# Reordering the first phase of a two-phase Mamba and attention kernel, with the moments of one norm moved from VectorE to ScalarE

## Chip, cores and metric

One NeuronCore of one Trainium2 chip. The metric is the device time of one execution in microseconds (us), lower is better. TensorE (PE), VectorE (DVE), ScalarE (ACT), GpSimd (POOL) and the DMA queue of SyncE (SP) run their own instruction streams and meet only at semaphores.

## The reference

Eight sequences of 512 tokens with 256 channels, all float32. Cut to what matters:

```
h  = layernorm(x, ln1_g, ln1_b)                        # "front" and x + h
xz = rmsnorm(h, rms_w) @ in_proj_w;  xi, z = split(xz) # "mid"
xc = silu(conv4(xi) + conv_b)
delta = softplus((xc @ x_proj_w)[:64] @ dt_proj_w + dt_proj_b)
scan over t: s = exp(delta*A) * s + delta*xc*B ;  y = sum(s*C) + D*xc
x  = x + h + (y * silu(z)) @ out_proj_w                # "back"
x  = x + relu(layernorm(x) @ w1 + b1) @ w2 + b2
g  = layernorm(x)                                      # "gate": an LSTM-like cell,
c  = sig(f)*c + sig(i)*tanh(..)                        # its state c runs from batch to batch
out term tanh(g @ wo + c @ uo + bo)
```

The second phase does attention (two units of eight heads for each batch) and a second pass of the same gate; at the end every batch's output is `x + tanh(xwo + c @ uo + bo)`.

## The kernel before

Everything is ordered by hand. The first phase (`sp_first`, `dve_first`, `act_first`, `pool_first`, `pe_first`) is a software pipeline: iteration `i` (0 to 9) runs the scan of batch `i` in 16 units `u`, and puts the other stages of its neighbours beside them at fixed `u`: `mid` of batch `i+1`, `front` (first norm) of `i+2`, `back` (output projection, FFN) of `i-1` and `gate` of `i-2`. Front exists for `i` = 0 to 5, gate from `i` = 2.

A scan unit is: POOL multiplies `ddb` by `bcb` into `hb` (`bx`, L1078, run three units ahead), ACT writes the exponentials to PSUM (`decay`, L872, one unit ahead), DVE scans (L615) and multiplies by C (L618; in units 4 and 12 POOL does it), and after four units PE sums over states (`sums`, L1199). `decay` of a unit waits until DVE has finished the unit two before it.

PE's matmuls of the other stages write to a ring of three PSUM banks (`first_uses`): the n-th use waits until the use n-3 has been read by its reader. In order: xi 2, out 2, gturn 2, xwo 2, gi 2, z 2, bturn 2, xp 1, FFN ... So `z`'s second half waits for ACT's reading of `gi`'s first (`gate_i`), the transposes `bturn` wait for the second `gi` and the first `z`, `xp` for the second `z`.

The moments of the first norm (`front_moments`) are on DVE at `u` = 6: four `bn_stats` (L501) and four `bn_aggr` (L505). POOL then makes the powers (`front_power`, L1027 to L1033), ACT applies them (`front_apply`, L783). The back norm has the same shape: DVE moments at `u` = 2, POOL `norm_power` (L1043 to L1048) at `u` = 2, ACT `back_apply` (L876) at `u` = 3, PE `bturn`, ACT `back_turned` (L888) at `u` = 6, then the FFN matmuls. POOL holds its large operations back during some of DVE's (the waits on `conv_ok`, `xc_ok`, `sz_ok`); `front_scale` (L1052, L1054) and DVE's `mid_soft` (L600, L602) had no such wait.

At the end DVE adds the final state term to `out_xwo` of each batch (`out_sum`, L1757, L1763), ACT takes the tanh, DVE adds it to `x` (`out_add`, L1769), SP stores.

## Time and profile before

| | us |
|---|---|
| median of 3 runs | 1586.55 (1586.42 to 1591.01) |
| the profiled execution, its time | 1584.47 |
| its span, first to last instruction | 1582.7 |
| PE busy | 1365.7 (86%) |
| DVE busy | 1195.4 (76%) |
| ACT busy | 880.1 (56%) |
| POOL busy | 674.7 (43%) |
| granted TensorE clock, mean | 0.939 |

The profile is of one execution; its own time is 2.1 us under the median and its span 1.8 us under its time. The first phase takes about the first 805 us. A busy share is an average over phases with different limits, so the table says little on what a change in one iteration is worth. Granted clock 1.00 is TensorE at 2.4 GHz, 0.50 at 1.2 GHz.

### The profile page before, as it was taken

To read this page: it belongs to the slowest core of one execution; us is meant where nothing else is said; L and a number is where in the kernel's file an instruction comes from. 1 tells how busy PE (TensorE), PEld (TensorE's weight loads), DVE (VectorE), ACT (ScalarE), POOL (GpSimd) and SP (SyncE) were. 2 spreads that over 40 slices of the span, in tenths; PEclk is the share of its full clock that TensorE was granted. 3 is DMA by queue.
4 is the path that set the end of the run, shared out by engine and by line. 5 is a ranking of instruction groups with operands and counts; after the bars stand their busy time and mean duration, and the time that the engine had idled before them with its cause. 6 is when DMAs were issued, how large, how long until landed. Compare 5 with 4: busy or idle time off the path is not lost.

```text
span 1582.7 us, 17383 instructions
## 1 busy us (share of the span) xinstructions
PE 1365.7 (86%) x5554; PEld 667.0 (42%) x5554; DVE 1195.4 (76%) x1861; ACT 880.1 (56%) x1514; POOL 674.7 (43%) x394
## 2 busy tenths in 40 slices
PE   7434889999999989799976989999999999999994
PEld 2102444545354545455541234454545444444442
DVE  5898999999999999880157878686877777776226
ACT  6465768585767665533112565656565655555633
POOL 2486979697978976731405131213022112100000
PEclk9666989999999999899986899999999999999997
DMA  6524161606161524300225352424343432330144
GB/s 209 188 72 169 60 206 42 215 29 212 55 213 55 186 69 140 100 14 27 66 79 128 79 122 52 99 49 106 71 95 71 95 78 62 75 69 2 42 157 136
DMA packets 93803, 158.05 MB, mean 100 GB/s; under 512 B 8608, under 2 KB 74720, under 8 KB 90592
## 3 DMA queue, kind: packets, MB, share of 16 engines
q1 hardware_dynamic: 93712, 156.94, 34.5%
q8 instruction: 45, 0.74, 0.2%
q14 instruction: 46, 0.38, 0.1%
HBM read 110.91 MB, written 46.01 MB: 99 GB/s over the span
## 4 chain that ended last, share of the span: by engine, by line
PE 59%; DVE 22%; issue 10%; ACT 4%; DMA 2%; POOL 2%; SPq 0%; DVEq 0%; POOLq 0%; ACTq 0%
PE psum L1149 24%; PE psum L2131 8%; PE psum L2065 7%; PE psum L2039 6%; PE psum L2054 5%; DVE psum L615 5%; DVE mx L1526 4%; PE psum L2009 4%; PE psum L1199 2%; DVE middle L579 1%; DVE hb L615 1%; POOL hb L1078 1%; DVE hb L618 1%; DVE bg_stats L501 1%; PE psum L1182 1%
## 5 line engine op out<-in xcount | busy, mean ns | idle before, releaser
L1526 DVE TENSOR_REDUCE mx<-psum 128x1 f32<-128x512 f32 x512 | 343.7, 685 | 151.6 <-PE psum L2039 150.4
L1785 ACT ACTIVATE pw<-psum 128x512 f32<-128x512 f32 x512 | 302.1, 598 | 274.2 <-PE psum L2054 270.8
L1078 POOL TENSOR_TENSOR hb<-ddb,bcb 128x1024 f32<-128x1024 f32 x127 | 309.4, 2458 | 79.8 <-DVE middle L579 55.4
L615 DVE TENSOR_TENSOR_SCAN psum<-psum,hb 128x512 f32<-128x512 f32 x224 | 261.6, 1213 | 26.6 <-ACT psum L872 15.8
L2039 PE MATMUL psum<-kp,qp 96*128 96x512 bf16 x512 | 203.7, 403 | 31.2 <-DVE mx L1526 21.4
L872 ACT ACTIVATE psum<-ddb,A_neg 128x512 f32<-128x512 f32 x256 | 165.3, 680 | 77.9 <-DVE hb L618 55.8
L2054 PE MATMUL psum<-qp,kp 99*128 99x512 bf16 x512 | 197.6, 387 | 5.0 <-ACT pw L1785 4.3
L1947 POOL TENSOR_TENSOR rstd<-rstd,neg_half 128x4 f32<-128x4 f32 x16 | 16.3, 1017 | 414.9 <-DVE rstd L1511 414.9
L618 DVE TENSOR_TENSOR hb<-psum,bcb 128x1024 f32<-128x1024 f32 x112 | 137.1, 1224 | 3.9
L2065 PE MATMUL psum<-pw,v_sb 128*32 128x512 f32 x1024 | 124.2, 602 | 0.5 <-ACT pw L1785 0.5
L1149 PE MATMUL psum<-back,w 128*128 128x512 f32 x256 | 115.3, 605 | 8.3 <-ACT back L888 8.3
L2039 PEld LDWEIGHTS psum<-kp,qp 96*128 96x128 bf16 x512 | 50.4, 99 | 143.1 <-DVE mx L1526 65.3
L2054 PEld LDWEIGHTS psum<-qp,kp 99*128 99x128 bf16 x512 | 49.5, 97 | 123.9 <-issue 91.2
L1199 PE MATMUL psum<-hb,sel 128*32 128x512 f32 x512 | 70.2, 672 | 32.4 <-DVE xc L627 22.3
L1149 PE MATMUL psum<-w,gate 128*128 128x256 f32 x384 | 88.1, 379 | 0.0
L1149 PE MATMUL psum<-late,wx 128*128 128x512 f32 x184 | 87.1, 596 | 0.0
L1149 PE MATMUL psum<-c_state,uh 128*128 128x512 f32 x184 | 86.5, 592 | 0.0
L2131 PE MATMUL psum<-second,wx 128*128 128x512 f32 x168 | 86.0, 592 | 0.0
L2131 PE MATMUL psum<-c_state,uh 128*128 128x512 f32 x168 | 85.8, 591 | 0.0
L1149 PEld LDWEIGHTS psum<-back,w 128*128 128x128 f32 x256 | 48.1, 192 | 75.0 <-issue 58.9
L1149 PEld LDWEIGHTS psum<-w,gate 128*128 128x128 f32 x384 | 73.0, 190 | 9.9
L1149 PE MATMUL psum<-front,w_in 128*128 128x512 f32 x128 | 62.6, 628 | 12.4 <-ACT late L915 8.8
(226 smaller groups left out, 2161.9 us busy)
## 6 DMA issues: line engine op xcount, KB each, us to landing
ddb<-dd SPq DMA_DIRECT2D x64, 512.0 KB, 6.7
bcb<-bc SPq DMA_DIRECT2D x32, 512.0 KB, 7.0
parts<-parts_sb SPq DMA_DIRECT2D x96, 128.0 KB
qp<-parts SPq DMA_DIRECT2D x32, 256.0 KB, 7.8
dd<-dd_out SPq DMA_DIRECT2D x7, 1024.0 KB, 4.8
kp<-parts SPq DMA_DIRECT2D x16, 384.0 KB, 4.6
x_back<-x_dram SPq DMA_DIRECT2D x9, 512.0 KB, 5.1
xh_back<-xh SPq DMA_DIRECT2D x8, 512.0 KB, 3.8
```

The source lines that it names most:

```text
L615: e.tensor_tensor_scan(to[:, g, :], a[:, g, :], h[:, g, :], 0.0, ALU.mult, ALU.add).then_inc(scan_ok, 1)
L618: e.tensor_tensor(h, a, bcb[q][:, 1, :, :], ALU.mult).then_inc(hc_dve, 1)
L872: e.activation(dA[n % 2][:, g, :], ddb[k % NSLOT][:, 0, :], ACT.Exp, scale=A_neg[:, a:a + 1]).then_inc(dA_ok, 1)
L1078: e.tensor_tensor(hb[n % NHB], ddb[k % NSLOT][:, 1:2, :].to_broadcast([P, 2, L]), bcb[q][:, 0, :, :], ALU.mult).then_inc(bx_ok, 2 if n == ...
L1149: ins = e.matmul(to, l, r, start=k == 0, stop=k == len(terms) - 1)
L1199: ins = e.matmul(bank(4)[jj * EB:(jj + 1) * EB, :], sel, h[:, g, :], start=(q == 0 and g == 0), stop=(q == 1 and g == 1))
L1526: used.up(e.tensor_reduce(mx[u % 2][:, n:n + 1], score_bank(used.n), AXIS.X, ALU.max))
L1785: e.activation(pw[n % NPW], bank(5 + n % 2), ACT.Exp, scale=HD ** -0.5).then_inc(exp_ok, 1)
L2039: used.up(e.matmul(score_bank(used.n), qp[u % 3][0:NROW, h, t * P:(t + 1) * P], kp[u % 3][0:NROW, h, :], start=True, stop=True))
L2054: e.matmul(bank(5 + n % 2), kp[u % 3][0:NROW + 3, h, kt * P:(kt + 1) * P], qp[u % 3][0:NROW + 3, h, :], start=True, stop=True).then_inc(st ...
L2065: ins = e.matmul(bank(7)[hh * VW:(hh + 1) * VW, :], v_sb[b % 2][:, kt, f * HU + q * 4 + hh, :], pw[(NSC * u + 4 * g + hh) % NPW], start=kt ...
L2131: ins = e.matmul(misc((name, b, f)), l, r, start=k == 0, stop=k == 3)
```

## The change

1. The moments of the first norm, from batch 2 on, leave DVE. ACT makes the sum of `x` in a pass with an accumulator (`front_mean`, `u` = 2), POOL turns it into minus the mean (`front_mean` of POOL, `u` = 3), and ACT makes the sum of squares in a second pass (`front_spread`, `u` = 3) that waits for POOL.
2. ACT: `decay` of the next batch's unit 0 before the end of the iteration; `gate_apply` at the end of the iteration before; `gate_turned` at `u` = 0; `gate_i` in two halves (`u` = 3, 4); `back_turned` at `u` = 5.
3. PE: the last `sums` of an iteration between the two halves of the transposes `fturn`; `gturn` ahead of `out`.
4. POOL: the second operation of `front_scale` waits for DVE's `mid_soft`.
5. End of the program: for the odd batches PE adds the terms into PSUM with an identity matrix, and ACT takes the tanh from there; DVE keeps the sums of the even ones.

```diff
@@ first_uses
         if mid:
             use("act", "xi", i + 1, 2)
+        if gate:
+            use("act", "gturn", i - 2, 2)
         if back:
             use("dve", "out", i - 1, 2)
         if gate:
-            use("act", "gturn", i - 2, 2)
@@ dve_first
-                    if u == 6 and front:
-                        front_moments(i + 2)
@@ act_first
+            def front_mean(b):
+                e.wait_ge(x_in[b % 2], 16 * (b // 2 + 1))
+                ring_done(e, "fturn", b - 1, 1)
+                for t in range(NT):
+                    ins = e.activation(tok(T0)[:, t, :], x_front[:, t, :], ACT.Identity, accum_out=f_sq[:, t:t + 1])
+                ins.then_inc(f_sum, 1)
+            def front_spread(b):
+                e.wait_ge(f_mean, b - 1)
+                for t in range(NT):
+                    ins = e.activation(tok(T0)[:, t, :], x_front[:, t, :], ACT.Square, bias=f_neg[:, t:t + 1], accum_out=f_mv[:, t, 1:2])
+                ins.then_inc(f_var, 1)
...
-                if s:
-                    decay(i, 0)
+                if i == 0:
+                    decay(0, 0)
                 for u in range(NUNIT):
                     if s and u + 1 < NUNIT:
                         decay(i, u + 1)
-                    if u == 0 and gate:
-                        gate_apply(i - 2)
+                    if u == 15 and i + 1 < NB:
+                        decay(i + 1, 0)
                     if u == 0 and mid:
                         mid_xi(i + 1)
-                    if u == 2 and gate:
+                    if u == 0 and gate:
                         gate_turned(i - 2)
+                    if u == 2 and front:
+                        front_mean(i + 2)
                     if u == 2 and gate and i <= NB:
                         gate_xwo(i - 2)
+                    if u == 3 and front:
+                        front_spread(i + 2)
+                    if u == 3 and gate:
+                        gate_i(i - 2, 0)
                     if u == 3 and mid:
                         mid_th(i + 1)
                     if u == 3 and back:
                         back_apply(i - 1)
                     if u == 4 and gate:
-                        gate_i(i - 2)
+                        gate_i(i - 2, 1)
                     if u == 5 and mid:
                         mid_z(i + 1)
                         mid_tz(i + 1)
-                    if u == 6 and back:
+                    if u == 5 and back:
                         back_turned(i - 1)
...
                     if u == 15 and front:
-                        front_turned(i + 2)
+                        front_turned(i + 2, (0,))
+                    if u == 15 and back:
+                        gate_apply(i - 1)
+                    if u == 15 and front:
+                        front_turned(i + 2, (1,))
@@ pool_first
+            def front_mean(b):
+                e.wait_ge(f_sum, b - 1)
+                e.tensor_scalar(f_neg, f_sq, -1.0 / D, None, ALU.mult).then_inc(f_mean, 1)
             def front_scale(b):
                 e.wait_ge(h_raw, b + 1)
                 own.up(e.tensor_tensor(tok(T0), tok(T0), over_tiles(row("ln1_g")), ALU.mult))
+                e.wait_ge(part_ok, 2 * b)
...
+                    if u == 3 and front:
+                        front_mean(i + 2)
+                    elif u == 9 and mid:
+                        e.wait_ge(part_ok, 2 * i + 4)
@@ pe_first
-                if back:
-                    sums(i - 1, 3)
                 if mid:
                     mid_in(i + 1, "xi", 0)
+                if gate:
+                    gate_turn(i - 2)
                 if back:
                     back_out(i - 1)
...
                 if front_:
-                    front(i + 2)
+                    front(i + 2, (0,))
+                if s:
+                    sums(i, 3)
+                if front_:
+                    front(i + 2, (1,))
@@ dve_second, act_second, pe_second (end of the program)
             out_sum(0)
-            out_sum(1)
+            out_sum(2)
             for b in range(NB):
-                if b + 2 < NB:
-                    out_sum(b + 2)
+                if b % 2 == 1 and b + 3 < NB:
+                    out_sum(b + 3)
                 out_add(b)
...
+                for u in range(2):
+                    e.wait_ge(out_pe, b + u + 1)
+                    ins = e.activation(y[:, 2 * u:2 * u + 2, :], halves(bank(OUT_BANKS[b // 2][u])), ACT.Tanh)
...
+            def out_xwo_term(b, u):
+                e.matmul(bank(OUT_BANKS[b // 2][u]), ident, out_xwo[b][:, 2 * u:2 * u + 2, :].rearrange("p t d -> p (t d)"), start=True, stop=False)
+            def out_state_term(b, u):
+                e.wait_ge(cuo_ok, 3 + u)
+                e.matmul(bank(OUT_BANKS[b // 2][u]), ident, cuo[:, 2 * u:2 * u + 2, :].rearrange("p t d -> p (t d)"), start=False, stop=True).then_inc(out_pe, 1)
```

Three places as they stand in the instruction order. First ACT in iteration 2, units 2 to 4 (`dd_out` is `mid_th`, `back0` is `back_apply`, `late1` is `gate_i`), before:

```order
L905 ACTIVATE late0<-psum 128x512 [waits r_pe] x2
L910 ACTIVATE gate2<-psum 128x512 [waits r_pe] x2
L872 ACTIVATE psum<-ddb4,A_neg 128x512 [waits hc_dve,dd_in4]
L872 ACTIVATE psum<-ddb4,A_neg 128x512
L833 ACTIVATE dd_out<-middle0 128x2x512 [waits dd_sent,conv_ok]
L876 ACTIVATE back0<-xh_back,bg_nb0,bg_rs0 128x256 [waits r_pe,b_rstd]
L876 ACTIVATE back0<-xh_back,bg_nb0,bg_rs0 128x256 x3
L872 ACTIVATE psum<-ddb5,A_neg 128x512 [waits hc_dve,dd_in5]
L872 ACTIVATE psum<-ddb5,A_neg 128x512
L915 ACTIVATE late1<-psum,half_bias 128x512 [waits r_pe] x2
```

The same place now:

```order
L790 ACTIVATE front0,f_sq<-x_front 128x256 [waits r_pe,x_in0]
L790 ACTIVATE front0,f_sq<-x_front 128x256 x3
L924 ACTIVATE gate2<-psum 128x512 [waits r_pe] x2
L886 ACTIVATE psum<-ddb4,A_neg 128x512 [waits hc_dve,dd_in4]
L886 ACTIVATE psum<-ddb4,A_neg 128x512
L797 ACTIVATE front0,f_mv<-x_front,f_neg 128x256 [waits f_mean]
L797 ACTIVATE front0,f_mv<-x_front,f_neg 128x256 x3
L928 ACTIVATE late1<-psum,half_bias 128x512 [waits r_pe]
L847 ACTIVATE dd_out<-middle0 128x2x512 [waits dd_sent,conv_ok]
L890 ACTIVATE back0<-xh_back,bg_nb0,bg_rs0 128x256 [waits r_pe,b_rstd]
L890 ACTIVATE back0<-xh_back,bg_nb0,bg_rs0 128x256 x3
```

The wait on `f_mean` now stands ahead of `mid_th`, `back_apply`, both halves of `gate_i` and the `decay` of unit 5.

POOL in the same iteration, from `norm_power` of the back norm on (`hb5` is `bx` of unit 5), before:

```order
L1043 TENSOR_SCALAR bg_rs0<-bg_mv0 128x4 [waits b_var]
L1044 TENSOR_SCALAR bg_neg0<-bg_mv0 128x4
L1046 TENSOR_TENSOR bg_rs0<-bg_rs0,neg_half 128x4 [waits pool_own]
L1048 TENSOR_TENSOR bg_nb0<-bg_neg0,bg_rs0 128x4 [waits pool_own]
L1078 TENSOR_TENSOR hb5<-ddb1,bcb1 128x1024 [waits bc_in1,sum_pe,dd_in1,conv_ok]
L1078 TENSOR_TENSOR hb6<-ddb2,bcb1 128x1024 [waits sum_pe,bc_in1,dd_in2]
```

The same place now:

```order
L1072 TENSOR_SCALAR bg_rs0<-bg_mv0 128x4 [waits b_var]
L1073 TENSOR_SCALAR bg_neg0<-bg_mv0 128x4
L1075 TENSOR_TENSOR bg_rs0<-bg_rs0,neg_half 128x4 [waits pool_own]
L1077 TENSOR_TENSOR bg_nb0<-bg_neg0,bg_rs0 128x4 [waits pool_own]
L1108 TENSOR_TENSOR hb5<-ddb1,bcb1 128x1024 [waits bc_in1,sum_pe,dd_in1,conv_ok]
L1062 TENSOR_SCALAR f_neg<-f_sq 128x4 [waits f_sum]
L1108 TENSOR_TENSOR hb6<-ddb2,bcb1 128x1024 [waits sum_pe,bc_in1,dd_in2]
```

The operation that releases ACT's second pass stands behind the whole `norm_power` and one `bx`.

PE at the start of iteration 2 (`front0` is `fturn`, `hb` is `sums`, `gate0` is `gturn`, `w_out` is `out`, `wo` is `xwo`), before:

```order
L1144 MATMUL psum<-ident,front0 128x128 [waits r_dve]
L1144 MATMUL psum<-ident,front0 128x128 x3
L1199 MATMUL psum<-hb4,sel 32x512 [waits hc_pool,hc_dve]
...
L1149 MATMUL psum<-w_out,xc1 128x256 [waits r_act,yT_ok]
...
L1144 MATMUL psum<-ident,gate0 128x128 [waits r_act,xr_ok]
L1144 MATMUL psum<-ident,gate0 128x128 x3
L1144 MATMUL psum<-ident,gate0 128x128 [waits r_dve]
L1144 MATMUL psum<-ident,gate0 128x128 x3
L1149 MATMUL psum<-wo,late0 128x256 [waits r_dve,r_act,w_gate]
```

and now:

```order
L1208 MATMUL psum<-front1,w_in 128x512 [waits r_act,r_dve]
L1208 MATMUL psum<-front1,w_in 128x512 [waits r_act] x3
L1178 MATMUL psum<-ident,gate0 128x128 [waits r_act,xr_ok]
L1178 MATMUL psum<-ident,gate0 128x128 x3
L1178 MATMUL psum<-ident,gate0 128x128 [waits r_act]
L1178 MATMUL psum<-ident,gate0 128x128 x3
L1183 MATMUL psum<-w_out,xc1 128x256 [waits r_act,yT_ok]
L1183 MATMUL psum<-w_out,xc1 128x256 x3
```

`gturn` stands where PE waited for `yT_ok`, and `sums` (not among these rows any more) stands ahead of the second half of `fturn`.

## Rows read from the trace of the kernel before

**Rows 1.** The chain that ended last: start us, length us, what.

```profile
412.51 16.11 PE psum L1149 x36
...
497.13 16.11 PE psum L1149 x36
```

**Rows 2.** Windows: length, busy us (instructions) per engine, granted clock, DMA share, GB/s.

```profile
412.60:497.20 84.60, 78.02 (x289) 41.45 (x289) 79.91 (x95) 58.80 (x101) 68.62 (x41) 1.00 0.37 126
156.70:160.40 3.70, 3.70 (x10) 1.00 (x12) 3.67 (x4) 2.46 (x4) 3.62 (x3) 0.50 0.00 0
```

**Rows 3.** TensorE in order of time; in brackets idle before, releaser.

```profile
462.48 0.65 PE L1144 MATMUL psum<-ident,front 128*128 128x128 f32 x4 [1.77 <-DVE c_state L670]
...
469.58 3.72 PE L1149 MATMUL psum<-w_out,xc 128*128 128x256 f32 x16 [0.97 <-DVE xc L627]
473.14 1.21 PE L1144 MATMUL psum<-ident,gate 128*128 128x128 f32 x8
475.49 3.72 PE L1149 MATMUL psum<-wo,late 128*128 128x256 f32 x16 [1.14 <-ACT late L905]
...
489.49 1.98 PE L1149 MATMUL psum<-front,w_in 128*128 128x512 f32 x4 [1.69 <-ACT late L915]
...
492.35 1.93 PE L1182 MATMUL psum<-xc,w_xp 128*96 128x512 f32 x4
494.21 1.92 PE L1199 MATMUL psum<-hb,sel 128*32 128x512 f32 x16
```

**Rows 4.** VectorE in order of time, same stretch.

```profile
414.38 1.39 DVE L501 BATCH_NORM_STATS2 f_stats<-x_front 128x6 f32<-128x256 f32 x4
...
432.30 2.41 DVE L600 SCALAR_TENSOR_TENSOR middle<-dd_out,middle 128x1024 f32<-128x1024 f32 x1 [0.16 <-ACT dd_out L856]
434.75 3.25 DVE L602 TENSOR_TENSOR middle<-middle 128x1024 f32<-128x1024 f32 x1
...
456.31 2.31 DVE L615 TENSOR_TENSOR_SCAN psum<-psum,hb 128x512 f32<-128x512 f32 x2
...
460.36 1.33 DVE L667 SCALAR_TENSOR_TENSOR psum<-psum,c_state 128x512 f32<-128x512 f32 x2 [0.47 <-PE psum L1149]
...
464.54 2.35 DVE L615 TENSOR_TENSOR_SCAN psum<-psum,hb 128x512 f32<-128x512 f32 x2 [1.52 <-ACT psum L872]
...
481.33 0.38 DVE L505 BATCH_NORM_AGGREGATE bg_mv<-bg_stats 128x2 f32<-128x6 f32 x4
```

**Rows 5.** ScalarE in order of time, same stretch.

```profile
425.80 2.06 ACT L783 ACTIVATE front<-x_front,f_nb,f_rs 128x256 f32<-128x256 f32 x4
...
442.72 0.41 ACT L795 ACTIVATE front<-front 128x256 f32<-128x256 f32 x1
...
483.95 1.06 ACT L833 ACTIVATE dd_out<-middle 128x1024 f32<-128x1024 f32 x1 [2.58 <-DVE middle L579]
485.13 2.08 ACT L876 ACTIVATE back<-xh_back,bg_nb,bg_rs 128x256 f32<-128x256 f32 x4
...
494.41 1.30 ACT L872 ACTIVATE psum<-ddb,A_neg 128x512 f32<-128x512 f32 x2 [1.12 <-DVE hb L618]
495.66 1.42 ACT L888 ACTIVATE back<-psum,vec 128x512 f32<-128x512 f32 x2
```

**Rows 6.** GpSimd in order of time, same stretch.

```profile
431.27 2.35 POOL L1054 TENSOR_TENSOR front<-front,rows 128x1024 f32<-128x1024 f32 x1
433.59 3.33 POOL L1078 TENSOR_TENSOR hb<-ddb,bcb 128x1024 f32<-128x1024 f32 x1
438.08 2.36 POOL L1064 TENSOR_TENSOR dd_out<-dd_out,middle 128x1024 f32<-128x1024 f32 x1 [1.16 <-DVE middle L602]
...
453.49 2.37 POOL L1078 TENSOR_TENSOR hb<-ddb,bcb 128x1024 f32<-128x1024 f32 x1
...
485.05 4.67 POOL L1078 TENSOR_TENSOR hb<-ddb,bcb 128x1024 f32<-128x1024 f32 x2
```

**Rows 7.** GpSimd in order of time, second iteration (i = 1).

```profile
148.48 4.67 POOL L1078 TENSOR_TENSOR hb<-ddb,bcb 128x1024 f32<-128x1024 f32 x2
```

**Rows 8.** TensorE in order of time, i = 1.

```profile
156.77 3.62 PE L1182 MATMUL psum<-xc,w_xp 128*96 128x512 f32 x4
...
162.33 7.13 PE L1149 MATMUL psum<-back,w 128*128 128x512 f32 x16
```

**Rows 9.** TensorE in order of time, i = 7.

```profile
637.23 6.05 PE L1149 MATMUL psum<-w_out,xc 128*128 128x256 f32 x16 [5.85 <-DVE xc L627]
...
661.29 15.70 PE L1149 MATMUL psum<-back,w 128*128 128x512 f32 x32 [3.09 <-ACT back L888]
```

**Rows 10.** TensorE in order of time, end of the program.

```profile
1552.28 3.62 PE L2009 MATMUL psum<-wo,second 128*128 128x256 f32 x16
```

**Rows 11.** VectorE in order of time, end of the program.

```profile
1560.11 3.50 DVE L1757 TENSOR_TENSOR out_xwo<-out_xwo,cuo 128x1024 f32<-128x1024 f32 x3
...
1577.21 1.22 DVE L1769 TENSOR_TENSOR x<-x,second 128x1024 f32<-128x1024 f32 x1
```

More of the change, by code:

```diff
@@ L172, in second_uses @@
     use(("gf", last, 1), "act")
-    use(("xwo", last, 0), "dve")
-    use(("xwo", last, 1), "dve")
     return place, who
@@ L803, in front_rms, with front_turned @@
                 ins.then_inc(m_ok, 1)
-            def front_turned(b):
-                for f in range(NF):
+            def front_turned(b, parts=range(NF)):
+                for f in parts:
                     ring_done(e, "fturn", b, f)
@@ L910, in gate_xwo, with gate_i @@
                     e.activation(tok(G2)[:, 2 * u:2 * u + 2, :], halves(ring("xwo", b, u)), ACT.Copy).then_inc(r_act, 1)
-            def gate_i(b):
-                for f in range(NF):
-                    ring_done(e, "gi", b, f)
-                    e.activation(feat(X1)[:, f, :], ring("gi", b, f), ACT.Tanh, bias=half_bias[:, 2 + f:3 + f], scale=0.5).then_inc(r_act, 1)
+            def gate_i(b, f):
+                ring_done(e, "gi", b, f)
+                e.activation(feat(X1)[:, f, :], ring("gi", b, f), ACT.Tanh, bias=half_bias[:, 2 + f:3 + f], scale=0.5).then_inc(r_act, 1)
             def gate_c(b):
@@ L1155, in token_product, with turned, front @@
                 return ins
-            def turned(name, b, src):
-                for f in range(NF):
+            def turned(name, b, src, parts=range(NF)):
+                for f in parts:
                     ring_free(e, name, b, f)
                     turn(tok(src), f, ring(name, b, f)).then_inc(r_pe, 1)
-            def front(b):
+            def front(b, parts=range(NF)):
                 e.wait_ge(m_ok, b + 1)
-                turned("fturn", b, T0 if b > 0 else mid0)
+                turned("fturn", b, T0 if b > 0 else mid0, parts)
             def mid_in(b, name, part):
@@ L1168, in mid_in @@
                     e.wait_ge(w_mamba, 64)
-                ring_out(e, "fturn", b, 1)
                 for f in range(NF):
@@ L1172, in mid_in @@
                     w = slice(part * D + f * P, part * D + (f + 1) * P)
-                    product(ring(name, b, f), [(w_in[:, k, w], feat(T1)[:, k, :]) for k in range(NF)]).then_inc(r_pe, 1)
+                    for k in range(NF):
+                        ring_out(e, "fturn", b, k)
+                        ins = e.matmul(ring(name, b, f), w_in[:, k, w], feat(T1)[:, k, :], start=k == 0, stop=k == NF - 1)
+                    ins.then_inc(r_pe, 1)
             def mid_xp(b):
@@ L1754, in out_sum @@
                     e.wait_ge(cuo_ok, 4)
[L1755 to L1764 removed]
+                e.wait_ge(out_in[b], 32)
+                e.tensor_tensor(out_xwo[b], out_xwo[b], cuo, ALU.add).then_inc(out_dve, 1)
             def out_add(b):
```

65 lines of the change are left out of this document (44 added, 21 removed).

## The prediction

> **What bounds the kernel now.** I read the chain of waits first. In iterations 2 to 5 it repeats every 84.62 us (412.51 to 497.13) and half of every period is one unbroken stretch of PE, the FFN and gate matmuls [rows 1]. The windows say that PE (78.02 us of 84.60) and DVE (79.91) are both nearly full there [rows 2], so the engine timelines must say who waits for whom. I count from F, the first FFN matmul of an iteration (412.51). PE runs without a wait until the gate's last matmul: DVE's `gate_state` begins at 460.36, F+47.85, after a wait for PE of only 0.47 [rows 4]. From there DVE leads: `gate_state` 2.66, an idle 1.52 for ACT's `decay` of unit 0 (which stands behind `front_turned`), the scan at 464.54, and scans, `back_sum`, conv up to the back norm's moments, which end at 481.71 [rows 4]. POOL's powers end at 485.05 [rows 6], ACT's `back_apply` starts at 485.13. ACT then reaches `back_turned` at 495.66, after `decay` of unit 7, which waited for DVE [rows 5], and PE starts the next FFN at 497.13. DVE + POOL + ACT lead for the first half of an iteration, PE for the second. PE's own waits in the first half are 1.77, 0.97, 1.14 and 1.69 [rows 3] and 1.0 at F.
>
> **The change part by part, in one steady iteration.**
>
> *DVE's moments leave.* 1.80 us (414.38 to the next operation's start at 416.2, [rows 4]). They lie between F and F+47.85, where DVE ends with 0.47 to spare against PE. Taking them away makes DVE wait longer for PE: 0 on the path. What hides this is PE's stretch.
>
> *POOL's `front_scale` waits for `mid_soft`.* DVE's two operations took 2.41 and 3.25; the first ended just after POOL's L1054 (433.62), the second after POOL's `bx` (436.92) [rows 4, 6]. So one excluded the other; the shortest run of such a shape that I allow is 1.2, and DVE gets back up to 3.2. The Trainium skill (GPSIMD Engine Reference, Key points) says that POOL shares its SBUF interfaces with VectorE and collides with DVE instructions of two SBUF inputs; the trace agrees with these two durations. By that rule alone the wait would be worth 3.2 us in every iteration. By the rows it is hidden too: it lies in PE's stretch. POOL pays: L1054 starts about 3.4 later, the `bx` behind it is 1.0 shorter, so `mid_du` (438.08) starts some 1.2 later and all behind it, down to the `bx` of unit 15 (453.49) and scan 15 (456.31) [rows 4, 6]. Scan 15 then ends near F+48.15: costs 0.3.
>
> *`decay` of unit 0 early, `sums` in the gap of `fturn`.* The idle 1.52 goes: the next scan starts at F+50.8 instead of F+52.03, a gain of 1.2.
>
> *`gturn` ahead of `out`, `gate_apply` early.* They fill PE's 0.97 and 1.14, which are not on the path in a steady iteration (DVE leads there). 0.
>
> *The two ACT passes.* This is the term that decides. ACT's `front_mean` lies in idle time of ACT and costs nothing. `front_spread` waits for POOL's small operation, and POOL comes to it only after `norm_power` and one `bx`. In the frame of F, with the scan at 50.8: the DVE stretch to the end of the moments is 17.17 (464.54 to 481.71): 67.95. `norm_power` with its hand-over 3.34 (to 485.05): 71.3. One `bx` is half of 4.67 [rows 6]: 73.65. POOL's operation on four columns and its semaphore, 0.3: 73.95. ACT has been free since about 67. `front_spread`: four passes with an accumulator took 0.40 each from start to start, four with bias and scale as columns 0.5 (2.06 for four, last one included) [rows 5]; I take 2.1, between 1.7 and 2.5. That gives 76.05. Queued behind it on ACT: half of `gate_i` 0.6, `mid_th` 1.06, `back_apply` 2.0, `decay` 5 1.25, the other `gate_i` 0.6, `decay` 6 1.25, `mid_z` 1.1: 83.9. Before, `mid_th` and `back_apply` started 4.7 to 6 earlier on this scale. PE waits for all of these: `z`'s second half for `gate_i`, `bturn` for `gate_i` and `back_apply`, `xp` for `mid_z`. Behind `mid_z` PE has `xp` 1.85 and `sums` 1.85 (492.35 to 496.1, [rows 3]): next F at 87.6. `back_turned`, moved to unit 5, is done at 86.3 and no longer on the path. The period is 87.6 against 84.62: **+3.0**. DVE's scan 5 also starts late, but has PE's stretch to catch up in.
>
> *The clock.* PE now idles some 4.5 us ahead of `z`'s second half and twice more until `xp`. The rows show what that does: in iteration 1, after a long wait for ACT, `xp` took 3.62 at a granted clock of 0.50 (1.2 GHz), against 1.93 at 1.00 (2.4 GHz) [rows 2, 3, 8]; in iteration 7 `out` took 6.05 after 5.85 idle, against 3.72, and the FFN 15.70 after 3.09 idle [rows 3, 9]. After the waits of 1.77 and less in the steady iteration nothing was slow. I take +1.7 for `xp` (bounds 0 and 3.5, if the FFN's start is slow as well). The Trainium skill (TensorE: Matmul & The Clock Gate, Why this matters for your kernels) asks that longer idle gaps between bursts of matmuls be avoided, and so speaks against this part of the change; by the rule the slow `xp` is to be expected, without it the sum would be 8.5 us lower. Steady total **+4.7** (bounds 3.0 and 6.5).
>
> **The sum.**
> - First iterations. At i = 0 there is no norm of `back` and ACT's wait ends before `mid_th` is needed. DVE gains 1.8 and 3.2, but POOL, not DVE, sets the end of it. At the start of i = 1 `xi` and `out` come 1.9 later, since the slow `sums` and half of `fturn` with ACT's reading stand ahead of them. Then the same chain from POOL's 148.48 (end of `norm_power`, [rows 7]): `bx` 2.35, 0.3, 2.1, `mid_th` 1.06, `back_apply` 2.0, two `decay` 2.5, `mid_z` 1.1, `xp` 3.62, `sums` 2.05 gives 165.6 for F against 162.33 [rows 8], 3.3. Together +5.2.
> - i = 2: the gain of 1.2 at the scan is not there (no `gate_state` before it), PE reaches `out` 2.9 later (`gturn` 1.1, half of `fturn` 0.6, ACT's reading of it and its hand-over 1.2), and DVE waits there. 2.9 + 3.0 + 1.2 for the chain as above, less 0.5 of slack, + 1.7 clock: +8.3.
> - i = 3, 4, 5: 3 x 4.7 = +14.1.
> - i = 6 has no front: the same chain without POOL's answer and the pass ends `mid_z` at 78.4 and gives F at 82.2, -2.4; gaps of 2 us before `bturn` and `xp` may slow PE a little: -1.5. i = 7: `back_turned` no longer behind `decay` 7, and `gturn` in PE's idle time of 5.85: PE's wait of 3.09 goes [rows 9], -3.0. i = 8: `gturn` with its waits off the path, -1.7.
> - End of the program. DVE's tail is bound by DVE: 16 operations of about 1.14 from 1560.11 to 1578.43 [rows 11]. Four are gone with the tile of the last batch (4.6 us); DVE starts 0.9 sooner, because the last `xwo` (3.62, [rows 10]) no longer stands ahead of `final_state`, two short products do. PE must do 12 products of 0.86 and the last `xwo` plus two, 10.3 + 5.3 after about 1554.1, less the two done before: until about 1572, so ACT's last tanh ends near 1572.9 and the last sum near 1574.1, against 1578.43. The loads are in by then. -4.3 (bounds 0, if PE is at 1.2 GHz there, and -5.5).
>
> 5.2 + 8.3 + 14.1 - 6.2 - 4.3 = +17.1. The profiled execution took 1584.47, which gives 1601.6; it lies 2.1 under the median of the runs, so against the median 1586.55 I say **1603.6**.
>
> **The rivals.** A move of 0.3%, 4.8 us, is about what a measurement of this kernel tells from no change.
>
> (a) *The clock stays at 2.4 GHz* after the new gaps: 1.7 less in four intervals and at F of i = 6: 1595. Part of my own range; about 0.2 of the chance.
>
> (b) *Faster: ACT's wait does not reach PE.* This is what the order aims at: a back half released sooner. It decides at conv's end, F+70.2: if POOL's answer were there by F+68, `front_spread` would be over when `mid_th` can start. Then each of i = 2 to 5 gives 2.4 (F at 82.2), i = 1 about 0 net, and the rest stays: -9.6 - 6.2 - 4.3 = -20, **1566**. For it: PE has 6.6 us of idle time in a period, all of it addressed. Against it: POOL takes instructions in order, and `norm_power` cannot start before DVE's moments end at 67.95. It would need a mistake in my placing of POOL's stream. 0.12.
>
> (c) *About the same*: the chain costs less than I count (`front_spread` 1.7, `back_apply` partly overlapped, no slow clock: +1.5 a period) and the end gives all: 5 + 6 + 4.5 - 6.9 - 5.5 = +3, 1590. 0.12.
>
> (d) *More than that*: the FFN's start is at 1.2 GHz as well and the end gives nothing: 4 x 1.8 + 4.3 more, 1615. 0.1.
>
> My forecast with (a) and (d) holds 0.76. The range of 80% is 1588 to 1614: it leaves out (b) and the edges of (c) and (d). Slower by over 0.3% (above 1591.3): 0.77. Within 0.3%: 0.1. Faster: 0.13.
>
> **What the profile of the changed kernel would show.** ACT idle some 6 us before L797, released by POOL's L1062, in every iteration from 1 to 5; right behind it the second `z` on PE. A period F to F near 89 (87.6 if the clock holds) in i = 3 to 5, and near 83 for i = 6. `xp` at 3.6 and a granted clock under 1.00 in the steady windows. DVE's L601 and L603 at about 1.2 each, with DVE then waiting for POOL's `bx` 13 and 15. No wait of DVE for `decay` of unit 0. At the end 12 DVE operations in the tail and PE busy to about 1572 plus the shift. I am wrong if L1062 stands before the `bx` in time, if the period is below 84.6, or if PE's stretch from F is no longer 47.8.

## The result: 11 us slower, inside the range

The changed kernel takes 1597.84 us in the median of 4 runs (1597.04 to 1598.37) against 1586.49 before (1583.01 to 1591.01, 4 runs on the same chip): a ratio of 1.0077, 95% interval 1.0057 to 1.0098. The forecast was 1603.6, range 1588 to 1614, slower with a chance of 0.77. The profiled execution has a span of 1596.2 against 1582.7, 13.5 more.

I measured every interval from F to F (first FFN matmul of an iteration) in both traces. "To F1" is from the start of the program.

| stretch | before | after | predicted | measured |
|---|---|---|---|---|
| to F1 | 162.33 | 167.07 | +5.2 | +4.7 |
| F1 to F2 (i = 2) | 80.93 | 91.49 | +8.3 | +10.6 |
| F2 to F5 (i = 3, 4, 5) | 253.87 | 267.26 | +14.1 | +13.4 |
| F5 to F6 | 84.64 | 84.52 | -1.5 | -0.1 |
| F6 to F7 | 79.52 | 75.78 | -3.0 | -3.7 |
| F7 to F8 | 71.26 | 67.16 | -1.7 | -4.1 |
| F8 to the last gate products | 809.43 | 806.79 | 0 | -2.6 |
| from there to the end | 40.72 | 36.13 | -4.3 | -4.6 |
| sum | 1582.7 | 1596.2 | +17.1 | +13.5 |

The windows of two steady iterations, which answer to [rows 2]: the length is 89.1 and 88.9 instead of 84.6, and the granted clock is no longer 1.00.

```profile
347.80:436.90 89.10, 80.94 (x293) 42.66 (x289) 75.99 (x87) 62.00 (x117) 66.67 (x40) 0.96 0.36 119
436.90:525.80 88.90, 81.48 (x292) 42.96 (x288) 75.91 (x87) 61.83 (x117) 66.73 (x40) 0.94 0.36 120
```

ScalarE and then GpSimd of the changed kernel in the second of these stretches (they answer to [rows 5, 6]). L797 is `front_spread`, L1062 the small operation `f_neg` for which it waits; L1072 is the first of `norm_power`.

```profile
503.46 1.30 ACT L886 ACTIVATE psum<-ddb,A_neg 128x512 f32<-128x512 f32 x2 [2.48 <-DVE hb L619]
511.02 0.51 ACT L797 ACTIVATE front<-x_front,f_neg 128x256 f32<-128x256 f32 x1 [6.25 <-POOL f_neg L1062]
...
513.57 1.04 ACT L847 ACTIVATE dd_out<-middle 128x1024 f32<-128x1024 f32 x1
514.52 2.06 ACT L890 ACTIVATE back<-xh_back,bg_nb,bg_rs 128x256 f32<-128x256 f32 x4
...
517.71 0.66 ACT L928 ACTIVATE late<-psum,half_bias 128x512 f32<-128x512 f32 x1
...
519.51 1.06 ACT L840 ACTIVATE sz<-psum 128x512 f32<-128x512 f32 x2
```

```profile
505.18 0.64 POOL L1072 TENSOR_SCALAR bg_rs<-bg_mv 128x4 f32<-128x4 f32 x1 [2.89 <-DVE bg_mv L506]
...
508.44 2.34 POOL L1108 TENSOR_TENSOR hb<-ddb,bcb 128x1024 f32<-128x1024 f32 x1
510.75 0.23 POOL L1062 TENSOR_SCALAR f_neg<-f_sq 128x4 f32<-128x4 f32 x1
```

ACT stands 6.25 us idle. ACT's sums for `f_neg` were complete at 499.40, but POOL first waits for `norm_power`, does it, and does a `bx` of 2.34. The back norm's `back_apply` could have started when POOL's powers were ready at about 508.5; it starts at 514.52.

TensorE of the same stretch (to [rows 3]):

```profile
513.72 3.78 PE L1208 MATMUL psum<-front,w_in 128*128 128x512 f32 x4 [4.79 <-ACT late L928]
518.52 1.09 PE L1178 MATMUL psum<-ident,back 128*128 128x128 f32 x4 [1.02 <-ACT late L928]
520.14 1.11 PE L1178 MATMUL psum<-ident,back 128*128 128x128 f32 x4 [0.53 <-ACT sz L840]
521.04 2.99 PE L1218 MATMUL psum<-xc,w_xp 128*96 128x512 f32 x4
```

The second half of `z` waits 4.79 and then takes 3.78 instead of 1.98, `xp` 2.99 instead of 1.93.

VectorE of the same stretch (to [rows 4]): the two operations of `mid_soft` take 1.23 and 1.22, scan 13 waits for a `bx`, and scan 0 (487.87) follows `gate_state` at once, at F+50.99.

```profile
456.68 1.23 DVE L601 SCALAR_TENSOR_TENSOR middle<-dd_out,middle 128x1024 f32<-128x1024 f32 x1 [0.16 <-ACT dd_out L870]
457.94 1.22 DVE L603 TENSOR_TENSOR middle<-middle 128x1024 f32<-128x1024 f32 x1
...
471.03 2.35 DVE L616 TENSOR_TENSOR_SCAN psum<-psum,hb 128x512 f32<-128x512 f32 x2 [1.48 <-POOL hb L1108]
...
485.34 1.29 DVE L668 SCALAR_TENSOR_TENSOR psum<-psum,c_state 128x512 f32<-128x512 f32 x2
486.67 1.29 DVE L671 SCALAR_TENSOR_TENSOR c_state<-psum,late 128x512 f32<-128x512 f32 x2
487.87 2.34 DVE L616 TENSOR_TENSOR_SCAN psum<-psum,hb 128x512 f32<-128x512 f32 x2
```

TensorE's last gate products and VectorE's last sum (to [rows 10, 11]). Before, the same group started at 1541.98.

```profile
1560.07 10.46 PE L2264 MATMUL psum<-second,wx 128*128 128x512 f32 x24
```

```profile
1591.02 1.23 DVE L1801 TENSOR_TENSOR x<-x,second 128x1024 f32<-128x1024 f32 x1 [1.00 <-ACT second L1957]
```

### The profile page after: what moved, and what is told of

Same layout as the page of the kernel before. It is cut to its first block, busy times and chain, and to the rows that moved or that the text cites. A ratio compares the mean times of both kernels' runs of the same rounds, so it can differ in the third digit from the quotient of the medians.

```text
span 1596.2 us, 17518 instructions
## 1 busy us (share of the span) xinstructions
PE 1388.3 (87%) x5582; PEld 674.9 (42%) x5582; DVE 1165.6 (73%) x1808; ACT 899.1 (56%) x1614; POOL 664.1 (42%) x394
## 4 chain that ended last, share of the span: by engine, by line
PE 60%; DVE 17%; issue 11%; ACT 5%; POOL 4%; DMA 3%; SPq 0%; POOLq 0%; ACTq 0%; DVEq 0%
PE psum L1183 22%; PE psum L2169 8%; PE psum L2103 7%; PE psum L2077 6%; PE psum L2092 5%; DVE mx L1566 4%; DVE psum L616 4%; PE psum L2047 4%; PE psum L1235 3%; PE psum L1218 1%; POOL hb L1108 1%; ACT psum L886 1%; DVE middle L580 1%; PE psum L2264 1%; ACT back L890 1%
## 5 line engine op out<-in xcount | busy, mean ns | idle before, releaser
L1566 DVE TENSOR_REDUCE mx<-psum 128x1 f32<-128x512 f32 x512 | 343.2, 685 | 151.1 <-PE psum L2077 150.0
L1108 POOL TENSOR_TENSOR hb<-ddb,bcb 128x1024 f32<-128x1024 f32 x127 | 298.8, 2373 | 78.0 <-DVE middle L580 50.6
L1208 PE MATMUL psum<-front,w_in 128*128 128x512 f32 x128 | 68.9, 681 | 22.9 <-ACT late L928 19.1
```

Source lines behind the costliest of these rows:

```text
L1108: e.tensor_tensor(hb[n % NHB], ddb[k % NSLOT][:, 1:2, :].to_broadcast([P, 2, L]), bcb[q][:, 0, :, :], ALU.mult).then_inc(bx_ok, 2 if n == ...
L1566: used.up(e.tensor_reduce(mx[u % 2][:, n:n + 1], score_bank(used.n), AXIS.X, ALU.max))
```

## The experiments

Each kernel was timed beside the kernel before on one chip. The period is the mean of the three intervals F2 to F5. "Soft wait" is short for POOL's wait for `mid_soft`. In the traces of before and of the run with the new end alone, whose first phase is the same code, F1 differs by 1.4 us, so a difference of one or two us at F1 tells nothing.

The intervals are of one profiled execution each, and it is not always a typical one: that of experiment 1 is 4.7 us above the median of its kernel, that of 5 is 6.0 above, that of 10 is 3.6 below. Experiments 1 to 4, 5 to 8 and 9 to 12 ran on three different chips, where the kernel before took 1586.7, 1588.4 and 1587.1, so totals of different groups are compared by their ratios.

| kernel | to F1 | F1 to F2 | period | F5 to F6 | F6 to F8 | median | ratio (95%) |
|---|---|---|---|---|---|---|---|
| before | 162.3 | 80.9 | 84.6 | 84.6 | 150.8 | | |
| changed | 167.1 | 91.5 | 89.1 | 84.5 | 142.9 | 1597.8 | 1.0077 (1.0057-1.0098) |
| 1 `f_neg` early | 166.3 | 86.0 | 85.0 | 85.3 | 143.3 | 1578.9 | 0.9944 (0.9928-0.9960) |
| 2 moments on DVE | 166.0 | 86.0 | 85.0 | 85.2 | 143.3 | 1582.6 | 0.9974 (0.9958-0.9991) |
| 3 passes, old order | 165.4 | 87.4 | 90.4 | 84.6 | 151.0 | 1609.7 | 1.0149 (1.0111-1.0186) |
| 4 new end alone | 163.7 | 81.0 | 84.6 | 84.6 | 150.8 | 1582.4 | 0.9968 (0.9951-0.9984) |
| 5 soft wait alone | 167.6 | 83.6 | 85.7 | 85.4 | 147.9 | 1590.6 | 1.0023 (1.0007-1.0039) |
| 6 `f_neg`, gate, z early | 162.5 | 83.2 | 83.9 | 81.7 | 151.3 | 1580.6 | 0.9955 (0.9940-0.9970) |
| 7 spread last | 165.2 | 86.0 | 85.0 | 85.3 | 143.3 | 1579.2 | 0.9946 (0.9929-0.9962) |
| 8 spread last, gate, z early | 162.6 | 85.0 | 83.6 | 81.9 | 151.1 | 1579.5 | 0.9948 (0.9933-0.9963) |
| 9 as 7, no soft wait | 160.6 | 85.3 | 84.1 | 84.8 | 143.3 | 1572.4 | 0.9915 (0.9890-0.9940) |
| 10 as 8, no soft wait, xc early | 157.3 | 83.8 | 83.0 | 83.0 | 149.4 | 1572.5 | 0.9911 (0.9888-0.9933) |
| 11 as 10, moments on DVE | 163.1 | 82.3 | 82.9 | 82.9 | 150.2 | 1573.3 | 0.9926 (0.9903-0.9950) |
| 12 changed, PE kept busy | 168.7 | 91.8 | 89.1 | 84.5 | 143.0 | 1599.7 | 1.0089 (1.0064-1.0113) |

**1. POOL's small operation one place earlier.**

```diff
                 for u in range(NUNIT):
+                    if u == 2 and front:
+                        front_mean(i + 2)
                     if u == 2 and back:
                         norm_power(0, b_var, i, b_rstd)
...
-                    if u == 3 and front:
-                        front_mean(i + 2)
```

> The changed kernel with one edit: POOL's small operation f_neg (L1062) stands one place earlier, ahead of norm_power and the bx behind it. Theory (ACT's front_spread holds ACT's queue because its input comes late from POOL's queue): POOL can answer at about 502.3 in the iteration that ran from 436.88, ACT is free for the passes at 504.8, they are over before mid_th can start, the wait of 6.3 us ahead of L797 is gone, PE's waits of 4.79 and 1.02 shrink to under 2, the period falls from 88.9 to 82 to 84 and the kernel takes 1566 to 1578 us. Rival (the passes' own 3.7 us of ACT are the price, whatever their place): the period stays above 87, 1590 or more. Rival (the new order of PE's queue and banks is the price): no change, 1597.

Faster than before and than the changed kernel: 1578.86, just above the 1566 to 1578 expected, and the period falls by 4.1. ScalarE, then TensorE, in the iteration from 422.05:

```profile
489.87 0.49 ACT L797 ACTIVATE front<-x_front,f_neg 128x256 f32<-128x256 f32 x1
...
493.68 2.08 ACT L890 ACTIVATE back<-xh_back,bg_nb,bg_rs 128x256 f32<-128x256 f32 x4
...
497.32 0.67 ACT L928 ACTIVATE late<-psum,half_bias 128x512 f32<-128x512 f32 x1
```

```profile
498.13 0.63 PE L1178 MATMUL psum<-ident,back 128*128 128x128 f32 x4 [2.32 <-ACT late L928]
500.19 1.11 PE L1178 MATMUL psum<-ident,back 128*128 128x128 f32 x4 [1.43 <-ACT sz L840]
501.10 3.62 PE L1218 MATMUL psum<-xc,w_xp 128*96 128x512 f32 x4
504.65 2.63 PE L1235 MATMUL psum<-hb,sel 128*32 128x512 f32 x16
```

L797 waits for nothing, and `back_apply` starts as soon as its own input is there. That rules out both rivals, the passes' own ACT time and the new order: the passes still run, and the new order of PE's queue is still there. But the period is 85.0 and not 82 to 84: PE still waits 2.32 for the second half of `gate_i`, which now stands behind `back_apply` and `decay` 5, and 1.43 for `mid_z`, and `xp` and `sums` behind these gaps take 2.4 more than in [rows 3] (1.4 to 2.5 over the five intervals from F1 to F6).

**2. The moments back on DVE, all else as changed.** `front_moments` at unit 6 for every batch again; the passes, `f_neg` on POOL and their waits are gone.

> The changed kernel with the moments of the first norm back on DVE at unit 6 for all batches; the new order and the new end stay. Theory: no wait of ACT for POOL, DVE's 1.80 us lie in PE's stretch and cost nothing, period 82 to 84, 1566 to 1578 us, within 3 us of the kernel with POOL's small operation early. Rival (passes' own ACT time is the price): also fast, and 5 us or more below the kernel with the early small operation. Rival (the new order is the price): 1595 to 1600.

From F1 on each interval is the same as in experiment 1 to 0.1 us. So the passes cost no time in the first phase where they don't wait, and the new order with the soft wait in it leaves the period nearly where it was (85.0 against 84.6). The total, 1582.57, misses both expectations (1566 to 1578, and within 3 us of experiment 1): the median is 3.7 above that of 1, where the profiled spans (1581.7 and 1581.5) don't differ. The profiled execution of 1 was the slowest of nine, so the traces can't say where the 3.7 lie. That the moments on DVE cost something outside the periods is not ruled out.

**3. The passes alone in the old order.** The kernel before with `front_mean` and `front_spread` on ACT at units 2 and 3 and `f_neg` at POOL's unit 3.

> The kernel before with only the two ACT passes in place of DVE's moments from batch 2 on, with POOL's small operation at unit 3 as in the change; old order, old end. Theory: ACT waits some 6 us ahead of front_spread, and the old order adds its wait for decay 0 and back_turned behind decay 7, so the period is 88.5 to 91, 1603 to 1618 us. Rival (the new order is the price): 1583 to 1589, a period near 84.6.

1609.68, period 90.4: as expected, and above the changed kernel. The old order adds its waits and the old end is kept, as the theory had it. ACT's wait is the same as in the changed kernel:

```profile
509.11 0.51 ACT L797 ACTIVATE front<-x_front,f_neg 128x256 f32<-128x256 f32 x1 [6.26 <-POOL f_neg L1057]
```

**4. The new end alone.**

> The kernel before with only the new end of the program (half of the last sums by PE). Theory: the end gives what the prediction said, 4.3 us: 1582.2, and every period of the first phase stays 84.6. Rival (the end gives nothing alone, because PE's products run at 1.2 GHz or the loads set it): 1586 to 1587.

1582.36 beside 1586.68: -4.3, as predicted, with an interval of -7.8 to -2.5, so the agreement to the tenth is luck.

**5. POOL's wait for `mid_soft` alone, in the kernel before.**

```diff
                 own.up(e.tensor_tensor(tok(T0), tok(T0), over_tiles(row("ln1_g")), ALU.mult))
+                e.wait_ge(part_ok, 2 * b)
                 e.wait_ge(own.sem, own.n)
...
                     if u == 9 and front:
                         front_scale(i + 2)
+                    elif u == 9 and mid:
+                        e.wait_ge(part_ok, 2 * i + 4)
```

> The kernel before with only POOL's wait for DVE's mid_soft between the two operations of front_scale (and in the iterations without a front, ahead of the next bx). As predicted: DVE's two operations of mid_soft fall from 2.41 and 3.25 to about 1.2 each, but the 3.2 us lie in PE's stretch; POOL runs 1.2 later behind it; period 84.6 to 85.0, 1586 to 1590 us. Rival (the freed port time is worth its 3.2 us an iteration): 1564. Rival (this wait is what costs the changed kernel its first two intervals): F of i = 1 at 165 or later, 1591 to 1596.

1590.64 beside 1588.37, 2.3 slower (interval 1.1 to 6.2), between the theory and the last rival. In the trace, which is of the slowest of ten executions, the period is 1.0 longer (0.3 predicted), and F1 to F2 2.7. VectorE, GpSimd and TensorE in the iteration from 422.43:

```profile
442.24 1.23 DVE L600 SCALAR_TENSOR_TENSOR middle<-dd_out,middle 128x1024 f32<-128x1024 f32 x1 [0.16 <-ACT dd_out L856]
443.50 1.23 DVE L602 TENSOR_TENSOR middle<-middle 128x1024 f32<-128x1024 f32 x1
...
456.60 2.35 DVE L615 TENSOR_TENSOR_SCAN psum<-psum,hb 128x512 f32<-128x512 f32 x2 [1.49 <-POOL hb L1079]
...
470.90 1.29 DVE L667 SCALAR_TENSOR_TENSOR psum<-psum,c_state 128x512 f32<-128x512 f32 x2
```

```profile
444.80 2.35 POOL L1055 TENSOR_TENSOR front<-front,rows 128x1024 f32<-128x1024 f32 x1 [4.08 <-DVE middle L602]
```

```profile
472.97 0.66 PE L1147 MATMUL psum<-ident,front 128*128 128x128 f32 x4 [2.34 <-DVE c_state L670]
473.55 3.43 PE L1202 MATMUL psum<-hb,sel 128*32 128x512 f32 x16
```

DVE's two operations are as short as they can be, and yet DVE gets to `gate_state` at F+48.47 instead of F+47.85: POOL was idle for 4.08, its `bx` come late, and scan 13 waits. PE's gap ahead of the second half of `fturn` grows from 1.77 [rows 3] to 2.34, and the `sums` behind it take 3.43 instead of 1.92 (2.93 to 3.44 in the four intervals from F2 to F6).

**6. Both halves of `gate_i` ahead of `mid_th`, and `mid_z` right behind `back_apply`**, on top of experiment 1.

```diff
                     if u == 3 and gate:
                         gate_i(i - 2, 0)
+                        gate_i(i - 2, 1)
...
                     if u == 3 and back:
                         back_apply(i - 1)
+                    if u == 3 and mid:
+                        mid_z(i + 1)
-                    if u == 4 and gate:
-                        gate_i(i - 2, 1)
                     if u == 5 and mid:
-                        mid_z(i + 1)
                         mid_tz(i + 1)
```

> The kernel with POOL's small operation early, and on ACT both halves of gate_i ahead of mid_th and mid_z right behind back_apply (ahead of decay 5). In the kernel with POOL's operation early alone, PE still waited 2.32 ahead of the first half of bturn for the second gate_i, and 1.43 ahead of the other for mid_z, and xp took 3.62 at a granted clock below 1.00. Theory (what is left is ACT's order, and the clock follows the gaps): both waits fall under 1 us, xp takes 1.93, F comes 4 to 5 us earlier until DVE limits, period 80 to 83, 1556 to 1572 us. Rival (DVE's chain of scans and not ACT's order sets it): PE waits elsewhere, period 84.5 or more, 1576 or more. Rival (the clock does not follow these gaps): waits under 1 us but xp still at 3.6.

The waits ahead of `bturn` are gone (0.26), but `xp` now waits for DVE's `mid_xc`, and the total is about that of experiment 1 (ratio 0.9955 against 0.9944). TensorE in two iterations in a row:

```profile
408.77 1.96 PE L1218 MATMUL psum<-xc,w_xp 128*96 128x512 f32 x4 [2.22 <-DVE xc L592]
...
492.17 3.19 PE L1218 MATMUL psum<-xc,w_xp 128*96 128x512 f32 x4 [2.22 <-DVE xc L592]
```

The total of 1580.6 misses the theory's 1556 to 1572 and lies in the first rival's range, though the period of 83.9 lies between the two: PE waits elsewhere, for DVE. The mean of 83.9 hides an alternation of 85.1, 81.7, 85.0 and 81.7. The gap of 2.22 stands ahead of `xp` every time, and yet `xp` takes 1.96 in three of the five intervals from F1 to F6, and 3.65 and 3.19 in the others. But `xp` starts every 83.4 us, whether the one before was slow or fast, so here a slow `xp` shifts one F and costs no period. The last intervals lose 8.0 of the 13.2 us that the trace is ahead of experiment 1 at F6 (F6 to F8 takes 151.3 instead of 143.3). In i = 7, with this order, ACT waits for PE's second `gi` product before it comes to `back_apply`, which starts 73.8 after F instead of 69.6. ScalarE in experiment 10, with the same order, and then in 9, with the old one:

```profile
646.56 0.69 ACT L928 ACTIVATE late<-psum,half_bias 128x512 f32<-128x512 f32 x1 [2.75 <-PE psum L1180]
647.14 2.06 ACT L890 ACTIVATE back<-xh_back,bg_nb,bg_rs 128x256 f32<-128x256 f32 x4
```

```profile
652.59 2.08 ACT L890 ACTIVATE back<-xh_back,bg_nb,bg_rs 128x256 f32<-128x256 f32 x4 [0.42 <-POOL bg_nb L1077]
...
655.80 0.67 ACT L928 ACTIVATE late<-psum,half_bias 128x512 f32<-128x512 f32 x1
```

**7. `front_spread` behind `back_turned` at unit 5; POOL untouched.**

> The changed kernel with POOL untouched and ACT's front_spread moved from the head of unit 3 to behind back_turned at unit 5. Theory (ACT's queue in order is the price, not the late answer itself): L797 waits for nothing, mid_th and back_apply start 4 to 5 us earlier, period 83.5 to 85.5, 1575 to 1584 us, as in the kernel with POOL's small operation early. Rival (the late variance itself costs, through front_power, front_norm and fturn): 1590 or more. Rival (the passes' own time of 3.7 us on ACT): 1590 or more, with the period above 87.

1579.2, with the intervals of experiment 1, as expected. POOL's answer is as late as in the changed kernel (it ends at F+74.1 in both) and costs nothing: when ACT comes to L797, some 6.8 us later, the answer is there. POOL and then ACT in the iteration from 420.93:

```profile
494.82 0.23 POOL L1062 TENSOR_SCALAR f_neg<-f_sq 128x4 f32<-128x4 f32 x1
```

```profile
501.84 0.50 ACT L797 ACTIVATE front<-x_front,f_neg 128x256 f32<-128x256 f32 x1
```

Together with 1 this settles the cause of the longer period.

**8. Experiments 6 and 7 together** (without the early `f_neg`).

> The changed kernel with front_spread behind back_turned, both halves of gate_i ahead of mid_th and mid_z right behind back_apply; POOL untouched. Theory: as the kernel with POOL's operation early and the same ACT order, within 4 us of it: 1556 to 1572, and front_spread's 2 us no longer ahead of mid_th give up to 1 us a period more. Rival (DVE's chain sets it): 1576 or more.

1579.46: within 4 us of experiment 6, as expected, but with it outside 1556 to 1572. `xp` waits 2.4 for DVE's `mid_xc`, as the rival had it.

**9. Experiment 7 without POOL's wait for `mid_soft`.**

> The kernel with front_spread behind back_turned (1579.2), without POOL's wait for mid_soft. Theory (from the wait put alone into the kernel before: a later POOL stream and slower matmuls behind PE's longer gap cost 1.2 us a period, and some 3 in the first interval): DVE's two operations of mid_soft go back to 2.4 and 3.2, the period falls from 85.1 to 83.6 to 84.4, F of i = 1 comes 2 to 4 earlier, 1568 to 1575 us. Rival (with decay 0 early, DVE and POOL have slack at that place and the wait is free): 1577 to 1582, period unchanged. Rival (the freed port time is worth something in the new order): slower, 1585.

1572.44, within the theory's range. Beside the kernel before on its chip this is 14.7 faster, against 9.2 with the wait (experiment 7). In the traces F1 comes 4.7 earlier and the period falls by 0.9. The wait is the second cost in the change. More than half of it falls before F1, where two executions of the same code already differ by 1.4.

**10. No soft wait, `gate_i` and `mid_z` early, and DVE's `mid_xc` ahead of scan 4.**

> The same without POOL's wait, with both halves of gate_i and mid_z early on ACT, and DVE's mid_xc ahead of scan 4 instead of behind it. With gate_i and mid_z early alone, PE waited 2.22 for mid_xc ahead of xp, and xp took 3.19. Theory (each gap of PE ahead of xp costs its length and a slow xp behind it): wait under 1 us, xp near 1.93, period 80 to 82.5, 1558 to 1569 us. Rival (scans and bx bound it by now): period 84 or more, 1573 or more.

TensorE in the iteration from 407.24:

```profile
483.21 1.14 PE L1175 MATMUL psum<-ident,back 128*128 128x128 f32 x8 [0.26 <-ACT back L890]
484.31 1.96 PE L1215 MATMUL psum<-xc,w_xp 128*96 128x512 f32 x4
486.20 1.92 PE L1232 MATMUL psum<-hb,sel 128*32 128x512 f32 x16
490.27 8.83 PE L1180 MATMUL psum<-back,w 128*128 128x512 f32 x16 [2.14 <-ACT back L902]
```

With no gap ahead of it `xp` takes 1.96, but `back_turned` is late behind two decays, and PE waits 2.14 ahead of the FFN. Here the 16 FFN matmuls behind that gap take 8.83 instead of 7.13. It is so in two of the five iterations from F2 to F6 (F2 and F5); in the other three the same gap leaves them at 7.29 to 7.46. All periods are 83.0 all the same, so the slow FFN costs nothing here, and what holds the period at 83.0 these runs don't show. The total, 1572.53, is that of 9, as the last intervals again take 6 more. Period and total missed my 80 to 82.5 and 1558 to 1569.

**11. The same with the moments on DVE.**

> The last kernel with the first norm's moments back on DVE at unit 6, no passes on ACT. As predicted for the kernel before (DVE's 1.80 us lie in PE's stretch and cost nothing): within 3 us of the last kernel. Rival (in an order in which PE waits less, DVE is the bound and its 1.80 us count in each of 4 or 5 periods): 6 to 9 us slower than the last kernel.

1573.27 and a period of 82.9: even here DVE's moments cost nothing in the period, and the median is 0.7 from that of 10, as expected. In the trace F1 comes 5.8 later and F8 4.4 later than in 10; whether that is the moments or the spread between executions, no run shows.

**12. PE kept busy in the gap.** In the changed kernel, the first half of `z` is computed three times over into the same bank, so the values stay the same.

```diff
+                    if name == "z" and f == 0 and 2 <= b < NB - 1:
+                        for _ in range(2):
+                            for k in range(NF):
+                                ins = e.matmul(ring(name, b, f), w_in[:, k, w], feat(T1)[:, k, :], start=k == 0, stop=k == NF - 1)
```

> The changed kernel with one edit on PE: in batches 2 to 6 the first half of z is computed three times over, into the same bank, so that some 3.5 of PE's 4.79 us of idle time ahead of z's second half are busy. Nothing else moves. Theory (the slow z half of 3.78 and xp of 2.99 come from PE's idle time): they take 1.98 and 1.93, sums follow, the period falls from 88.9 to 87.3 to 88.2, 1590 to 1595 us. Rival (the slow matmuls do not hang on this gap): the same durations and 1597. Rival (z's second half was late enough that its slow run was hidden and xp's gap stays slow): z at 1.98, xp still near 3, 1596 to 1598.

TensorE (L1212 are the added products):

```profile
510.75 3.60 PE L1212 MATMUL psum<-front,w_in 128*128 128x512 f32 x8
515.71 1.98 PE L1208 MATMUL psum<-front,w_in 128*128 128x512 f32 x4 [1.37 <-ACT late L928]
520.51 0.63 PE L1178 MATMUL psum<-ident,back 128*128 128x128 f32 x4 [2.82 <-ACT late L928]
522.13 1.12 PE L1178 MATMUL psum<-ident,back 128*128 128x128 f32 x4 [0.99 <-ACT sz L840]
523.04 3.01 PE L1222 MATMUL psum<-xc,w_xp 128*96 128x512 f32 x4
```

The slow half of `z` is fast again, and nothing is gained: its 1.8 us were covered by ACT, and now PE waits 2.82 instead of 1.02 ahead of `bturn`. The second rival holds in its durations (1599.68 is a little above its 1596 to 1598): `xp` takes 3.62, 3.23 and 3.01 in the three steady intervals, beside 3.61, 3.19 and 2.99 in the changed kernel. So the idle time ahead of `z` alone is not what makes it slow. That the gaps right ahead of `bturn` are, this run does not show by itself, since one of them grew; experiment 10, where they are gone, has `xp` at 1.96 in all five.

## Why the prediction came out as it did

**The ACT passes: right, in place and size.** `front_spread` waits for `f_neg` behind `norm_power` and one `bx`: 6.25 predicted as some 6. POOL's operation ends at F+74.1 (predicted 73.95), the passes take 1.98 (2.1), `mid_z` ends at F+83.7 (83.9), F comes at 88.9 (89.3 with the clock). Experiments 1 and 7, two different edits that both end this wait, each give 4.1 us a period back; experiment 3 puts the passes with this wait alone into the kernel before and costs 5.8 a period.

**The moments on DVE: right for the period.** 0 on the path. Experiments 2 and 11, with the moments on DVE, show the same period as 1 and 10 without them. For the whole program the medians leave 3.7 and 0.7 us open.

**POOL's wait for `mid_soft`: wrong size.** "Costs 0.3" was the step. The rows came out as worked out (the operations at 1.23 and 1.22; `mid_du` at F+26.98, 1.4 later). `gate_state` is late by 0.6 and not 0.3, and left out was that PE's gap behind it grows and that the matmuls behind the longer gap are slow: in the traces +1.0 a period alone (experiment 5), 0.9 in the new order (7 against 9), and 4.7 to F1. By the medians the wait costs 2.3 us alone and some 5 to 6 in the new order. The Trainium skill (GPSIMD Engine Reference, Key points) tells of the collision between POOL and DVE instructions of two SBUF inputs. The trace agrees with it in the durations, 2.41 and 3.25 against 1.23 and 1.22; but experiments 5 and 9 decide against its use here, where the wait that avoids the collision costs more than the collision.

**The first interval: right sum by luck, wrong parts.** "`xi` and `out` come 1.9 later" did not show: with the new order and neither of the two waits (experiment 9) F1 is at 160.6, not later than before. The soft wait alone gives +5.3 and the passes alone +3.1; together +4.7. That both lie on one chain, so that neither adds fully to the other, is my reading and not tested.

**i = 2: +10.6 against +8.3.** The new order with neither wait takes 85.3, +4.4 where my terms for the order (2.9 + 1.2 - 0.5) give 3.6. The rest is split by the runs as 0.7 for the soft wait (86.0 against 85.3) and 5.5 for the ACT wait (91.5 against 86.0), which I had at 4.7 with the clock.

**The clock: right in kind and size, not in its cause.** I took +1.7 on `xp` as a consequence of ACT's wait, and rival (a) as the case without it. In the three steady intervals `xp` took 3.61, 3.19 and 2.99, 1.7, 1.3 and 1.1 more than 1.93. With the second half of `bturn`, slow in the last two, that is 1.5 to 1.7 between `bturn` and F. The +1.8 on `z` experiment 12 shows to be hidden. But in experiment 1, with ACT's wait gone, `xp` still takes 3.62 behind gaps of 2.32 and 1.43: this price belongs to the new order of `gate_i` on ACT, and it goes only when these gaps do (experiment 10). The Trainium skill (TensorE: Matmul & The Clock Gate, Why this matters for your kernels) asks to avoid long idle gaps between bursts; the trace agrees in direction, with slow matmuls behind gaps of about 2 us and more, though not behind every one (last section). Experiment 12 adds that filling the longest gap was worth nothing here, as PE then waited longer at the next one. Rival (d), a slow start of the FFN, did not come in the changed kernel: its first 16 matmuls take 7.13 as before.

**Rival (b), and i = 6: too optimistic.** I worked out F at 82.2 for an iteration without ACT's wait. It is 85.0 in experiments 1, 2 and 7, and 84.5 for i = 6 in the changed kernel (F5 to F6). Missed was that the first half of `bturn` needs the bank of the second `gi`, and so ACT's second `gate_i`, which stands behind `back_apply` and `decay` 5. My steady sum had it in the queue, this case had not. Nor did 82.2 come as a steady period where `gate_i` was early: there `xp` starts every 83.4 us (experiment 6) or 83.6 (8). i = 7 and 8 gave 7.8 where I said 4.7. Most of the difference is i = 8: before, `out` waited 2.34 and then took 5.41; now it waits 0.36 and takes 3.72, and this change of speed was not in my term.

**The end: right, with a term missing in print.** -4.3 predicted, -4.3 by experiment 4, -4.6 in the trace. PE's terms as printed (1554.1 + 10.3 + 5.3, less two products of 0.86) end at 1568 and not at 1572; the product with `uo` that stands between them, 3.72 in the trace, is not among them. With it they end at 1571.7. In the trace PE ends at 1590.35, which is 1572.3 when counted from the last gate products as before.

**Why the total is 6 too high.** 1.0 of it is in the terms up to F8 and at the end, where misses of both signs cancel, and 2.6 in the second phase, whose code is the same: the shift falls there between 941 and 1017 us, in a stretch with a granted clock of 0.98 against 0.96 before. In the traces of experiments 2 and 4 the same stretch shifts by +0.6, so executions differ there by some 3 us. The last 2.1 I added for the distance between the profiled execution and the median, and the changed kernel's median is not above its own profiled execution (1598.04).
